# Moving an unused 480-byte gap from in front of the streamed weight sums to in front of the ring of operands

## The chip, the cores and the metric

The kernel runs on one core of one Trainium2 chip. The metric is the device time of one execution in microseconds (us), lower is better. Times of a kernel are medians of several executions; the profile shows one more execution of its own.

## The reference

The reference is one transformer layer in float32 on x of shape (4, 1024, 256): attention with 16 heads of 16 and binarised weights, then a feed-forward part with ternary weights. The feed-forward part is what the change touches:

```python
def _tlin(x, w, s):
    return jnp.einsum('bsi,oi->bso', x, w) * s
h = jax.nn.silu(_tlin(x, w1_w, w1_s)) * _tlin(x, w2_w, w2_s)     # 256 -> 1024
h = jax.nn.gelu(_tlin(h, h1_w, h1_s), approximate=False)         # 1024 -> 1024
h = jax.nn.gelu(_tlin(h, h2_w, h2_s), approximate=False)         # 1024 -> 1024
return _tlin(h, w3_w, w3_s)                                      # 1024 -> 256
...
x = x + _layernorm(_L0_attn_ref(_layernorm(x, axis=-1), ...), axis=-1)
x = x + _layernorm(_L0_ffn_ref(_layernorm(x, axis=-1), ...), axis=-1)
```

## The kernel before

The kernel has three parts, one after the other: `project` (the first tokens' projections), `attention` (the rest of it, about half of the time) and `tail_ffn` (output projection, layer norms and the feed-forward part). The tiles that the change moves exist only in `tail_ffn`; no tile of the first two parts changes its place.

`tail_ffn` goes through the 4096 tokens in 8 blocks of 512. TensorE runs an order of work that is written out by hand (`step`): 16 tiles of the first layer (`first_tile`, lines 1831 and 1832), then for each of the two hidden 1024 x 1024 layers 7 products of half size by Strassen's scheme in Winograd's form (`product`, line 1893), then the last layer (`out_part`, line 1906). In the first hidden layer the output projection of the next block (`project_y`, line 1798) stands between two products, and 8 transposes (`turn_x1`, line 1806) stand inside the last layer.

Numbers with all bits of float32 are given to TensorE as a high and a low part (tile `op_hi`, and `op_lo` as the rest), so each weight tile is used by two matmuls in a row. ScalarE makes `op_hi` (line 2008), VectorE makes `op_lo` (line 2148), into a ring of three slots each, 4096 bytes per partition and slot. One product is 32 matmuls (2 halves, 4 k-tiles, 2 output tiles, 2 parts), each with a stationary tile of 128x128 and a moving tile of 256 columns:

```python
w = weights(l, k, kt, 2 * h + a)
for part in (op_hi, op_lo):
    mm = pe.matmul(dst[:, a * HB:(a + 1) * HB], w, part[slot][:, kt // 2, cols].bitcast(form), ...)
```

With 14 products in each of 8 blocks that makes 14 x 32 = 448 matmuls of line 1893 in a block and 3584 in the program. 4 of 7 products read their weights from `W`, which stays in SBUF; 3 of 7 read them from `sums_of_w`, two tiles of 8192 bytes that are streamed from DRAM by SyncE's queue.

A trace writes the moving operand first and the stationary one second: `ffn_ps<-op_hi,W` is a matmul whose moving operand is `op_hi` and whose weights come from `W`. In line 1906 the roles are exchanged (`ffn_ps<-W,op_hi`): there `op` is stationary and `W` moves.

**Where the tiles lie.** The program allocates SBUF in order, each tile after the one before it; the byte address in each partition follows from the sizes. Slices are whole multiples of 512 bytes from their tile's start (128 columns of 4 bytes), so what can tell two uses apart is the start modulo 512:

```
tile                       start     modulo 512   used by TensorE in lines
signs_p                    16512     128          1798 (moving)
W                          24736     160          1831, 1832, 1893 (stationary), 1906 (moving)
x_hi0 of project           82592     160          697 (moving)
x2_hi, x2_lo               131232    160          1831, 1832 (moving), 1798, 1203, 1205 (stationary)
feed0, feed1               143552    192          -
op_hi0..2, op_lo0..2       176320    192          1893 (moving), 1906 (stationary)
gap (480 bytes, unused)    200896    -            -
sums_of_w0, sums_of_w1     201376    160          1893 (stationary)
signs                      223200    480          697, 698 (stationary), 1203, 1205 (moving)
```

(In the trace the names `x_hi` and `x_lo` stand for `x2_hi` and `x2_lo` too, which `attention` uses in lines 1203 and 1205.)

Of the kernel before, what the change touches and what calls it, by code (L numbers as in the profile page):

```python
# [6 lines left out]
F32 = mybir.dt.float32  # L7
# [7 lines left out]
P = 128  # L15
# [216 lines left out]
def layer(nc, x, attn_w, attn_wT, attn_b, attn_b_rows, ffn_w, ffn_s, ffn_s3, out):  # L232
# [14 lines left out]
    with ExitStack() as keep, ExitStack() as until_ffn:  # L247
# [57 lines left out]
        attention(nc, c, qk_scr, v_scr, m_scr, y_scr, ffn_w, w_scr, sum_scr, W, quads, first, x, tail_in, inv_scr, spent)  # L305
        until_ffn.close()
        tail_ffn(nc, x, y_scr, sum_scr, inv_scr, c, W, tail_in, out)


# [1260 lines left out]
def tail_ffn(nc, x, y_scr, sum_scr, inv_scr, const, W, tail_in, out):  # L1570
# [9 lines left out]
    with ExitStack() as ctx:  # L1580
        def sb(name, shape, dt):
            return ctx.enter_context(nc.sbuf_tensor(name, shape, dt))
# [6 lines left out]
        y_hi, y_lo = x2_hi, x2_lo  # L1589
        feed = [sb(f"feed{l}", [P, 4, 2, BLK], F32) for l in range(LAYERS)]  # L1590
        RING = 3
        op_hi = [sb(f"op_hi{r}", [P, 2, BLK], F32R) for r in range(RING)]
        op_lo = [sb(f"op_lo{r}", [P, 2, BLK], F32R) for r in range(RING)]
        SHIFTED = 480
        sb("gap", [P, SHIFTED // 4], F32)
        sums = [sb(f"sums_of_w{u}", [P, HK, HM], F32R) for u in range(2)]
        gate = [sb(f"gate{a}", [P, BLK], F32) for a in range(2)]
        o_sb = sb("o_sb", [P, TILES, DIM], F32)
# [80 lines left out]
        def op_at(i, l, k):  # L1679
            return OPS * i + NP * l + k + 1  # L1680
# [109 lines left out]
        def _(pe):  # L1790
# [87 lines left out]
            def product(i, l, k):  # L1878

                slot, fresh = (NP * l + k) % RING, k in (K_C11, K_C11_END, K_Z)  # L1880
                pe.wait_ge(op_lo_done, op_at(i, l, k))
# [17 lines left out]
            def out_part(i, dst, r, s, a, first, last):  # L1899
# [5 lines left out]
                for part in (op_hi, op_lo):  # L1905
                    mm = pe.matmul(dst, part[o % RING][:, s // 2, tokens].bitcast(form), w,  # L1906
                                   start=(first and part is op_hi), stop=(last and part is op_lo))
# [60 lines left out]
        def _(act):  # L1968
# [22 lines left out]
            def wait_slot(i, o):  # L1991

                old = o - RING if o >= RING else o - RING + OPS
                old_i = i if o >= RING else i - 1
                if isinstance(old_i, int) and old_i < 0:
# [385 lines left out]
```

## Time and profile before

| what | value |
|---|---|
| median of 3 runs | 1169.46 us (1166.7 to 1173.56) |
| the profiled execution's own time | 1167.74 us |
| its span, first to last instruction | 1166.0 us |
| granted TensorE clock, mean | 0.992 of full speed |
| TensorE busy | 1130.3 us, 97% of the span |
| ScalarE busy | 922.5 us, 79% |
| VectorE busy | 749.4 us, 64% |

The profiled execution took 1.74 us more than its span (what lies before the first and after the last instruction). Matmuls are pipelined: each is recorded with its whole passage (some 280 ns for 256 columns), and the next one starts before it has ended. What a matmul costs is therefore the distance from its start to the next one's start, which this text calls its step; it is read from the chain (length of a piece by its count) or from start times in the timeline.

### The profile page before, as it was taken

What the parts mean: (1) busy time and instruction counts of PE and PEld (TensorE: products, weight loads), DVE (VectorE), ACT (ScalarE), POOL (GpSimd) and SP (SyncE); (2) the same over time, 40 slices, a digit from 0 to 9 for tenths busy, and PEclk for the clock granted to TensorE, in tenths of its full rate; (3) what the DMA queues carried; (4) which work ended last, traced back from release to release, by engine and by line L of the source; (5) the groups of instructions that cost most, each with busy time, mean ns of one, the idle gap of its engine ahead of it and who ended that gap; (6) DMA issues with size and microseconds to landing.
All of it is one profiled execution on the core that took longest, in us unless ns stands there. A gap on an engine that the chain in (4) does not pass through costs nothing.

```text
span 1166.0 us, 21113 instructions
## 1 busy us (share of the span) xinstructions
PE 1130.3 (97%) x8241; PEld 769.6 (66%) x8241; DVE 749.4 (64%) x1162; ACT 922.5 (79%) x1218; POOL 97.0 (8%) x140
## 2 busy tenths in 40 slices
PE   6699999999999999998999999999999999999997
PEld 4233333333333322324999999999999999999997
DVE  8354524363345436795876878768778687687666
ACT  6689999999999999996676676667756766677665
POOL 6001000101010100010010000010100000101000
PEclk9799999999999999999999999999999999999999
DMA  5989768996879859954332430433324314333031
GB/s 187 242 213 236 189 101 188 219 224 105 166 166 198 178 97 224 266 159 174 109 110 76 145 128 22 153 137 109 113 71 145 128 32 168 113 109 131 15 127 56
DMA packets 67319, 167.03 MB, mean 143 GB/s; under 512 B 10390, under 2 KB 27414, under 8 KB 61062
## 3 DMA queue, kind: packets, MB, share of 16 engines
q1 hardware_dynamic: 66924, 165.18, 52.9%
q8 instruction: 70, 1.15, 0.4%
q10 hardware_dynamic: 288, 0.39, 0.2%
q14 instruction: 37, 0.30, 0.1%
HBM read 122.21 MB, written 52.43 MB: 150 GB/s over the span
## 4 chain that ended last, share of the span: by engine, by line
PE 52%; DVE 1%; issue 0%; ACT 0%; ACTq 0%
PE ffn_ps L1893 36%; PE ffn_ps L1831 5%; PE ffn_ps L1832 5%; PE ffn_ps L1906 5%; PE side_ps L1798 1%; PE side_ps L1806 1%; DVE ln_stats L2242 0%; DVE o_sb L2253 0%; DVE o_sb L2250 0%; DVE o_sb L2240 0%; ACT op_hi L2008 0%; DVE ln_mean_var L2244 0%; DVE ln_rstd L2248 0%; DVE op_lo L2148 0%; ACTq L2001 0%
## 5 line engine op out<-in xcount | busy, mean ns | idle before, releaser
L1308 ACT ACTIVATE probs<-s_ps 128x1024 f32<-128x1024 f32 x512 | 475.3, 1140 | 29.0 <-PE s_ps L1153 28.2
L1167 PE MATMUL y_ps<-probs,v_st 128*17 128x512 f32 x2048 | 270.3, 600 | 4.3 <-ACT probs L1308 2.1
L1893 PE MATMUL ffn_ps<-op_hi,W 128*128 128x256 f32 x1024 | 240.4, 279 | 0.0
L1893 PE MATMUL ffn_ps<-op_lo,W 128*128 128x256 f32 x1024 | 240.4, 279 | 0.0
L1153 PEld LDWEIGHTS s_ps<-q_st,k_st 50*128 50x128 f32 x1024 | 88.1, 185 | 208.9 <-ACT probs L1308 171.9
L2148 DVE TENSOR_TENSOR op_lo<-feed,op_hi 128x1024 fp32r<-128x1024 f32 x144 | 175.3, 1222 | 67.7 <-ACT op_hi L2008 67.6
L1153 PE MATMUL s_ps<-q_st,k_st 50*128 50x512 f32 x1024 | 207.1, 469 | 8.4 <-DMA q_st<-shift 7.9
L1893 PEld LDWEIGHTS ffn_ps<-op_lo,W 128*128 128x128 f32 x1024 | 192.6, 188 | 0.3
L1893 PEld LDWEIGHTS ffn_ps<-op_hi,W 128*128 128x128 f32 x1024 | 192.4, 188 | 0.3
L2008 ACT ACTIVATE op_hi<-feed 128x1024 fp32r<-128x1024 f32 x144 | 151.2, 1055 | 50.0 <-DVE feed L2166 21.9
L1893 PE MATMUL ffn_ps<-op_lo,sums_of_w 128*128 128x256 f32 x768 | 180.7, 279 | 0.0
L1893 PE MATMUL ffn_ps<-op_hi,sums_of_w 128*128 128x256 f32 x768 | 180.6, 279 | 0.0
L1893 PEld LDWEIGHTS ffn_ps<-op_lo,sums_of_w 128*128 128x128 f32 x768 | 144.5, 188 | 0.0
L1893 PEld LDWEIGHTS ffn_ps<-op_hi,sums_of_w 128*128 128x128 f32 x768 | 144.3, 188 | 0.0
L2037 ACT ACTIVATE feed<-feed,scales 128x256 f32<-128x256 f32 x192 | 86.9, 501 | 29.8 <-DVE feed L2191 15.1
L1831 PE MATMUL ffn_ps<-x_hi,W 128*128 128x512 f32 x256 | 99.8, 390 | 2.8 <-issue 2.8
L1832 PE MATMUL ffn_ps<-x_lo,W 128*128 128x512 f32 x256 | 99.7, 389 | 0.0
L1975 ACT ACTIVATE gate<-ffn_ps,scales 128x512 f32<-128x512 f32 x64 | 43.9, 688 | 64.3 <-PE ffn_ps L1832 64.3
L1167 PEld LDWEIGHTS y_ps<-probs,v_st 128*17 128x17 f32 x2048 | 34.5, 95 | 82.0 <-issue 72.6
L1333 DVE COPY y_sb<-y_ps 128x512 f32<-128x512 f32 x32 | 22.1, 690 | 103.1 <-PE y_ps L1167 103.1
L2141 DVE SCALAR_TENSOR_TENSOR feed<-ffn_ps,scales,gate 128x512 f32<-128x512 f32 x64 | 47.0, 747 | 32.3 <-PE ffn_ps L1832 32.3
L1906 PE MATMUL ffn_ps<-W,op_hi 128*128 128x256 f32 x256 | 62.0, 284 | 0.6 <-DVE op_lo L2148 0.6
(207 smaller groups left out, 1310.0 us busy)
## 6 DMA issues: line engine op xcount, KB each, us to landing
sums_of_w<-sum_scr SPq DMA_DIRECT2D x48, 1024.0 KB, 5.1
k_st<-qk_scr SPq DMA_DIRECT2D x90, 128.0 KB, 6.6
q_st<-qk_scr SPq DMA_DIRECT2D x90, 128.0 KB, 7.1
w_scr<-ffn_w SPq DMA_DIRECT2D x16, 704.0 KB, 7.8
W<-w_scr SPq DMA_DIRECT2D x16, 704.0 KB, 5.9
y_scr<-y_sb SPq DMA_DIRECT2D x32, 256.0 KB, 2.9
qk_scr<-y SPq DMA_DIRECT2D x24, 256.0 KB, 6.8
qk_scr<-sums SPq DMA_DIRECT2D x24, 256.0 KB, 7.7
```

The costliest lines, as they stand in the source:

```text
L1153: i = pe.matmul(s_ps[a % 3][:, hh, :], k_st[u][rows, pp, s * P:(s + 1) * P], q_st[u][rows, pp, tb * BLK:(tb + 1) * BLK], start=True, stop= ...
L1167: i = pe.matmul(y_ps[32 * j:32 * j + VCOLS, :], v_st[g % 2][:, s, VCOLS * j:VCOLS * (j + 1)], probs[(PAIRS * turn + j // 2) % PROBS][:, j ...
L1308: act.activation(probs[a % PROBS][:, :, :], s_ps[a % 3][:, :, :], ACT.Exp, scale=SCALE)\
L1831: pe.matmul(dst, w, x2_hi[:, c, :].bitcast(form), start=(c == 0), stop=False)
L1832: mm = pe.matmul(dst, w, x2_lo[:, c, :].bitcast(form), start=False, stop=(c == CT - 1))
L1893: mm = pe.matmul(dst[:, a * HB:(a + 1) * HB], w, part[slot][:, kt // 2, cols].bitcast(form), start=(fresh and kt == 0 and a == 0 and part ...
L1906: mm = pe.matmul(dst, part[o % RING][:, s // 2, tokens].bitcast(form), w, start=(first and part is op_hi), stop=(last and part is op_lo))
L1975: act.activation(gate[n % 2][:, :], bank[BANK_ORDER[2 * n % 6]][:, :], ACT.Silu, scale=scales[:, S1_AT + n:S1_AT + n + 1]).then_inc(gate_d ...
L2008: act.activation(op_hi[o % RING][:, :, :], operand(o), ACT.Copy).then_inc(op_hi_done, 1)
L2037: g = act.activation(dst[:, cols], src[:, cols], ACT.Gelu, scale=scales[:, at:at + 1])
L2141: dve.scalar_tensor_tensor(dst, bank[BANK_ORDER[(2 * n + 1) % 6]][:, :].rearrange("p (j t) -> p j t", j=2), scales[:, S2_AT + n:S2_AT + n ...
L2148: dve.tensor_tensor(op_lo[o % RING][:, :, :], operand(o), op_hi[o % RING][:, :, :].bitcast(F32), ALU.subtract)\
```

## The change

The 480 bytes that no instruction reads or writes are allocated ahead of the ring `op_hi`, `op_lo` and no longer behind it. The ring's six slots lie 480 bytes higher (176800 and not 176320, so 160 and not 192 modulo 512). `sums_of_w` and all tiles behind it stay where they were, as do `W`, `feed` and all tiles ahead of the ring. No instruction, wait, semaphore or transfer is added, removed or put in another order.

```diff
         feed = [sb(f"feed{l}", [P, 4, 2, BLK], F32) for l in range(LAYERS)]
         RING = 3
+        SHIFTED = 480
+        sb("gap", [P, SHIFTED // 4], F32)
         op_hi = [sb(f"op_hi{r}", [P, 2, BLK], F32R) for r in range(RING)]
         op_lo = [sb(f"op_lo{r}", [P, 2, BLK], F32R) for r in range(RING)]
-        SHIFTED = 480
-        sb("gap", [P, SHIFTED // 4], F32)
         sums = [sb(f"sums_of_w{u}", [P, HK, HM], F32R) for u in range(2)]
```

## Rows read from the trace of the kernel before

**Rows 1.** The page, part 1: engine, busy us (share of the span), instructions.
```profile
PE 1130.3 (97%) x8241; PEld 769.6 (66%) x8241; DVE 749.4 (64%) x1162; ACT 922.5 (79%) x1218; POOL 97.0 (8%) x140
```

**Rows 2.** The chain that ended last, one block: start us, us, what, count.
```profile
558.35 18.67 PE ffn_ps L1893 x160
577.01 1.88 PE side_ps L1798 x16
578.90 33.61 PE ffn_ps L1893 x288
612.50 3.78 PE ffn_ps L1906 x32
616.29 0.87 PE side_ps L1806 x8
617.16 3.79 PE ffn_ps L1906 x32
...
635.50 18.67 PE ffn_ps L1893 x160
```

**Rows 3.** Windows of two whole blocks: stretch, us, then busy us of each engine.
```profile
558.33:635.48 77.15, 77.15 (x603) 74.62 (x602) 57.72 (x79) 51.74 (x82) 7.07 (x12) 1.00 0.30 104
...
635.48:712.63 77.15, 77.15 (x603) 74.61 (x602) 58.86 (x80) 53.70 (x86) 7.14 (x12) 1.00 0.33 111
```

**Rows 4.** Groups by line from 543.5 us on: busy, mean ns | idle before.
```profile
L1893 PE MATMUL ffn_ps<-op_hi,W 128*128 128x256 f32 x1024 | 240.4, 279 | 0.0
L1893 PE MATMUL ffn_ps<-op_lo,W 128*128 128x256 f32 x1024 | 240.4, 279 | 0.0
...
L1893 PE MATMUL ffn_ps<-op_lo,sums_of_w 128*128 128x256 f32 x768 | 180.7, 279 | 0.0
L1893 PE MATMUL ffn_ps<-op_hi,sums_of_w 128*128 128x256 f32 x768 | 180.6, 279 | 0.0
L2148 DVE TENSOR_TENSOR op_lo<-feed,op_hi 128x1024 fp32r<-128x1024 f32 x144 | 175.3, 1222 | 67.7 <-ACT op_hi L2008 67.6
L2008 ACT ACTIVATE op_hi<-feed 128x1024 fp32r<-128x1024 f32 x144 | 151.2, 1055 | 50.0 <-DVE feed L2166 21.9 <-DVE feed L2141 17.7 <-DVE feed L2159 5.2
...
L1906 PE MATMUL ffn_ps<-W,op_hi 128*128 128x256 f32 x256 | 62.0, 284 | 0.6 <-DVE op_lo L2148 0.6
```

**Rows 5.** Timeline of TensorE in a product, W and then sums_of_w stationary.
```profile
799.79 0.28 PE L1893 MATMUL ffn_ps<-op_lo,W 128*128 128x256 f32 x1
...
800.73 0.28 PE L1893 MATMUL ffn_ps<-op_lo,W 128*128 128x256 f32 x1
800.85 0.28 PE L1893 MATMUL ffn_ps<-op_hi,sums_of_w 128*128 128x256 f32 x1
...
802.95 0.28 PE L1893 MATMUL ffn_ps<-op_hi,sums_of_w 128*128 128x256 f32 x1
```

**Rows 6.** Timeline of TensorE in the first layer, 512 columns.
```profile
547.76 0.39 PE L1831 MATMUL ffn_ps<-x_hi,W 128*128 128x512 f32 x1
...
549.12 0.39 PE L1831 MATMUL ffn_ps<-x_hi,W 128*128 128x512 f32 x1
```

**Rows 7.** Timeline of TensorE in project, 512 columns.
```profile
20.29 0.39 PE L697 MATMUL qk_ps<-x_hi,signs 128*128 128x512 f32 x1
...
21.69 0.39 PE L697 MATMUL qk_ps<-x_hi,signs 128*128 128x512 f32 x1
```

**Rows 8.** Timeline of TensorE in attention, two times the same work.
```profile
213.44 0.28 PE L1205 MATMUL p_ps<-signs,x_lo 128*128 128x256 f32 x1
...
214.12 0.28 PE L1205 MATMUL p_ps<-signs,x_lo 128*128 128x256 f32 x1
...
209.00 0.28 PE L1205 MATMUL p_ps<-signs,x_lo 128*128 128x256 f32 x1
...
209.71 0.28 PE L1205 MATMUL p_ps<-signs,x_lo 128*128 128x256 f32 x1
```

**Rows 9.** Lines 2048 and 2199: min/median/max ns of writes into x2_hi, x2_lo.
```profile
L2048 ACT ACTIVATE x_hi<-y x7: 1044/1046/1049, 570.6 to 1033.5; 128x1024 fp32r<-128x1024 f32 x7
...
L2199 DVE TENSOR_TENSOR x_lo<-y,x_hi x7: 1224/1226/1227, 571.7 to 1034.6; 128x1024 fp32r<-128x1024 f32 x7
```

## The prediction

> **What bounds the kernel now.** I read the page first: TensorE is busy for 97% of the span, VectorE and ScalarE for 64% and 79% [rows 1]. Then the chain that ended last. From 543.5 us on it is TensorE alone, piece after piece without a gap, until the last layer norm; one block is 18.67 + 1.88 + 33.61 + 3.78 + 0.87 + 3.79 us and the first layer's 14.5 us, and the next block starts its products 77.15 us later [rows 2]. The windows of two blocks say the same: TensorE busy in all of the 77.15 us, VectorE in 58.9, ScalarE in 53.7 [rows 3], and the groups show no idle time ahead of line 1893 and 0.6 us in all ahead of line 1906 [rows 4]. So in this part of the program the time is the number of matmuls times their step, and no wait of another engine decides. The change can only count if it alters the duration of instructions: it moves no work and no order.
>
> Next, the steps. In the products a piece of 288 matmuls takes 33.61 us and one of 160 takes 18.67 us: both 116.7 ns each [rows 2]. 256 columns at the full clock of 2.4 GHz would be 106.7 ns, so each step holds 10.0 ns more. The timeline shows the same step with `W` (8 steps in 0.94 us, 117.5, rounded) and with `sums_of_w` (18 steps in 2.10 us, 116.7) [rows 5]. All ring slots, k-tiles and output tiles lie in these pieces, and the step is the same for all; so if the address counts, it is by what they have in common: the place modulo 512 bytes.
>
> **The change part by part.** (1) Moved: the six slots of the ring, from 192 to 160 modulo 512. Let D be the start of the stationary operand less that of the moving one, modulo 512. For the 3584 matmuls of line 1893 D is 160 - 192 = -32 before and 0 after. For the 512 of line 1906 (op stationary, `W` moving) it is 192 - 160 = +32 before and 0 after. Lines 1798, 1831 and 1832 keep their D (+32 and 0). (2) Not changed: `sums_of_w` and what lies behind it, and all DMAs, waits and queues.
>
> What does the step depend on? The trace has these classes:
> - 256 columns, D = -32: 116.7 ns, 10.0 over the columns' time [rows 2].
> - 256 columns, D = +32: line 1906 takes 3.78 us for 32, 118.1 ns; line 1798, with other tiles (moving at 128, stationary at 160), 1.88 us for 16, 117.5 ns [rows 2]. Between 0.8 and 1.4 ns above the products.
> - 256 columns, D = 160 - 480 = +192: the same code in two states, 6 steps in 0.68 us (113.3 ns) and 6 in 0.71 us (118.3 ns) [rows 8].
> - 512 columns, D = 0: 6 steps in 1.36 us, 226.7 ns, 13.3 over 213.3 [rows 6].
> - 512 columns, D = 480 - 160 = -192: 6 steps in 1.40 us, 233.3 ns, 20.0 over 213.3 [rows 7].
>
> The two 512-column classes have the same shape and the same kind of loop (a weight tile used for a high and a low part), and differ by 6.7 ns a step. The operands' places are the visible difference, which makes me believe that D counts at all; the steady levels stand 3.3 ns apart or a multiple of it (113.3, 116.7; 226.7, 233.3). I take it that the reading of the next weights and the reading of the moving columns get in each other's way, more or less according to D.
>
> The price of D = 0 with 256 columns is in no row, so it is bounded. Below: the shortest step of that width, 113.3 ns [rows 8], is also half of the 512-column step at D = 0 (226.7 / 2 = 113.3) [rows 6]; if the extra time goes with the columns, each matmul gains 3.33 ns, 3584 x 3.33 = 11.9 us less. Above: if the extra time belongs to one weight load (128 columns of weights in both widths), it is 13.3 ns here as in rows 6, so 106.7 + 13.3 = 120.0 ns, 3584 x 3.33 = 11.9 us more. Between: the neighbour at D = +32 is 1.4 ns dearer than the one at D = -32, 3584 x 1.4 = 5.0 us if D = 0 behaves like it. I take the upper value. With 256 columns the weight load, which overlaps the matmul before it, has no slack left: a disturbed load holds up the next matmul, whereas with 512 columns it is hidden, so the narrow matmul should pay at least what the wide one pays. It is also the next level above the present one.
>
> Line 1906 goes from 118.1 to 120.0 as well: 512 x 1.9 = 1.0 us more (below: 512 x 4.8 = 2.5 us less). Sum: 11.9 + 1.0 = 12.9 us.
>
> What is written to the ring costs nothing in either case. The 144 writes each of ScalarE (1055 ns) and VectorE (1222 ns) [rows 4] have twins that write into tiles at 160 modulo 512 from an unmoved source: 1046 and 1226 ns [rows 9], 9 ns less and 4 ns more; all of it lies under TensorE, with 77.15 - 58.86 = 18.3 us of room on VectorE in a block [rows 3]. If that cover were gone, it would be 144 x 4 ns = 0.6 us. Even with a TensorE block 1.5 us shorter (448 x 3.33 ns) VectorE stays under it, so a gain would arrive in full.
>
> A page of the Trainium skill speaks against all this. TensorE: Matmul & The Clock Gate, section Back-to-back issue gap, has a step of the columns at 2.4 GHz and some 2.5 ns, with no term for an address; by it the step would be an estimated 109.2 ns before and after and the sum zero. The trace does not agree with its size (116.7 ns) [rows 2], nor with one extra for both 512-column classes [rows 6, 7]. SBUF — State Buffer, section SBUF: two separate sides, says that TensorE's reads never wait for another engine; that fits the even steps, and would leave the ring's move without effect on what ScalarE and VectorE do to TensorE.
>
> **The sum against the times.** The profiled execution took 1167.74 us; 1167.74 + 12.9 = 1180.6 us. The median of the runs shown is 1.7 us above it, 1182.3 us with the same sum. I say 1180.5.
>
> **The rivals.**
> - The step rises, but only to that of the neighbours at D = +32: 3584 x 1.4 = 5.0 us, 1173 us. For it speak the two lines of that class [rows 2]; against it that they don't hold one level, as the steady classes do.
> - No change: D does not set the step, but the loop's order, or the state that a stretch falls into (the same code gave 113.3 and 118.3 ns [rows 8], with D the same). Time 1167.7 to 1169.5 us. For it: `W` and `sums_of_w` cost the same; but they have the same D. Against it: rows 6 against rows 7.
> - The other side: faster. The two read streams are best aligned when they start at the same place, and the extra goes with the columns: steps of 113.3 ns, 11.9 us less in line 1893 and 2.5 us less in line 1906, 14.4 us, 1153.3 us; with line 1893 alone 1155.8 us. For it: rows 6 have the lower of the two 512-column levels, and 113.3 is a state that does occur. It decides once the mean step of line 1893 falls below 115.0 ns (3584 x 1.63 = 5.8 us, 0.5%).
>
> **How the numbers follow.** Full rise to 120 ns: 0.42. Small rise, by 2 to 8 us: 0.16. No change: 0.22. Faster: 0.20. A measurement of this kernel can tell about 0.5% (5.8 us) from no change. Slower by over 0.5%: the 0.42 and 0.06 of the small rises, 0.48. Within 0.5%: 0.22 and the other 0.10 of the small rises, 0.32. Faster: 0.20. The range goes from 1157 us, which takes in most cases of a gain in line 1893 alone, to 1186 us, the likeliest case on the median (1182.3) and the spread of the runs; the likeliest one's own range is 1176 to 1186 us.
>
> **What would show it.** In the chain of the changed kernel the piece of 160 matmuls of line 1893 tells all: 18.67 us now, 19.20 us if the step is 120.0, 18.13 us if it is 113.3; the block of 77.15 us becomes 78.8 or 75.4. The first layer's pieces of 226.7 ns, line 1798, and everything ahead of 543.5 us should not move. The prediction is wrong if the step stays at 116.7 ns, or if `W` and `sums_of_w` get different steps, which would mean that it isn't D that counts; and it fails on its sign if the extra goes with the columns.

## The result, and the profile after

| | before | after |
|---|---|---|
| median of 6 runs each | 1168.28 us | 1182.03 us |
| the profiled execution's own time | 1167.74 us | 1181.85 us |
| its span | 1166.0 us | 1180.1 us |

The ratio is 1.0101, 95% interval 1.0079 to 1.0122: the kernel became slower by 1.0%. The forecast was 1180.5 us.

The page of the kernel after, part 1 (engine, busy us, share of the span, instructions), against [rows 1]:

```profile
PE 1145.5 (97%) x8241; PEld 783.7 (66%) x8241; DVE 749.7 (64%) x1162; ACT 923.8 (78%) x1218; POOL 96.8 (8%) x140
```

The instructions are the same in number; TensorE is busy for 15.2 us more, VectorE and ScalarE for 0.3 and 1.3 us more. The chain that ended last, one block of the kernel after (start us, us, what, count), against [rows 2]:

```profile
796.16 19.19 PE ffn_ps L1893 x160
815.35 1.90 PE side_ps L1798 x16
817.25 34.54 PE ffn_ps L1893 x288
851.79 3.84 PE ffn_ps L1906 x32
855.64 0.87 PE side_ps L1806 x8
856.51 3.83 PE ffn_ps L1906 x32
...
874.87 19.19 PE ffn_ps L1893 x160
```

The reader is to divide: 19.19 us by 160 and 34.54 us by 288 are 119.9 ns, where there were 116.7. Line 1906 went from 3.78 and 3.79 us to 3.84 and 3.83. Line 1806 and the first layer kept their times, and line 1798 (1.90 us for 1.88) nearly so. The timeline of one product after, 18 steps from its 13th matmul on:

```profile
640.00 0.28 PE L1893 MATMUL ffn_ps<-op_hi,W 128*128 128x256 f32 x1
...
642.16 0.28 PE L1893 MATMUL ffn_ps<-op_hi,W 128*128 128x256 f32 x1
```

2.16 us for 18 steps: 120.0 ns. (Start times are printed to 0.01 us, so a step read over 18 of them is good to some 0.6 ns.) A window of 78.7 us, which is a block of the kernel after, against [rows 3]:

```profile
721.00:799.70 78.70, 78.70 (x602) 76.19 (x601) 58.88 (x81) 53.86 (x87) 7.12 (x12) 1.00 0.32 109
```

TensorE is still without a gap, VectorE and ScalarE do the same work in more time. The difference of the spans is 14.1 us. It is made of 7 blocks that begin 78.71 us and not 77.15 us apart (10.9 us), the 448 matmuls of the last block in 53.75 and not 52.27 us (1.5 us), and 1.7 us by which the first product begins later (560.02 for 558.35 us). The last part is no work of the change. Windows of both kernels at the start of the first layer (the last three columns are the granted clock, the DMA share and GB/s); before:

```profile
540.00:545.00 5.00, 2.18 (x14) 1.24 (x7) 0.69 (x1) 1.51 (x2) 0.17 (x3) 1.00 0.45 128
545.00:550.00 5.00, 5.00 (x23) 4.13 (x22) 1.50 (x2) 1.84 (x3) 0.00 (x0) 1.00 0.91 365
```

and after:

```profile
540.00:545.00 5.00, 2.19 (x15) 1.08 (x8) 0.69 (x1) 1.28 (x1) 0.17 (x3) 0.84 0.40 108
545.00:550.00 5.00, 5.00 (x20) 4.02 (x19) 1.50 (x2) 1.38 (x2) 0.00 (x0) 0.81 0.95 379
```

TensorE was busy for less than half of the first of these windows in both (2.18 and 2.19 of 5.00 us), and in the execution profiled after it was granted the lower of its two clocks, 1.2 GHz, for some 3 us. Five steps of the first layer took 0.43 us each there, which is 512 columns at 1.2 GHz:

```profile
544.39 0.63 PE L1832 MATMUL ffn_ps<-x_lo,W 128*128 128x512 f32 x1
...
546.53 0.56 PE L1831 MATMUL ffn_ps<-x_hi,W 128*128 128x512 f32 x1
```

The experiments below show that this isn't the work of the change: the profiled executions of eight of their twelve kernels had such a stretch at this place and four had none, and the two kernels with the whole ring at D = +64 and +320, which are alike in all else, are one of each (granted clock 0.68 and 1.00 from 545 to 550 us).

### The profile page after: what moved, and what is told of

Read it like the earlier page. It is cut to its first block, busy times and chain, and to the rows that moved or that the text cites. A ratio compares the mean times of both kernels' runs of the same rounds, so it can differ in the third digit from the quotient of the medians.

```text
span 1180.1 us, 21113 instructions
## 1 busy us (share of the span) xinstructions
PE 1145.5 (97%) x8241; PEld 783.7 (66%) x8241; DVE 749.7 (64%) x1162; ACT 923.8 (78%) x1218; POOL 96.8 (8%) x140
## 4 chain that ended last, share of the span: by engine, by line
PE 53%; DVE 1%; issue 0%; ACT 0%; ACTq 0%
PE ffn_ps L1893 36%; PE ffn_ps L1831 5%; PE ffn_ps L1832 5%; PE ffn_ps L1906 5%; PE side_ps L1798 1%; PE side_ps L1806 1%; DVE ln_stats L2242 0%; DVE o_sb L2253 0%; DVE o_sb L2250 0%; DVE o_sb L2240 0%; ACT op_hi L2008 0%; DVE ln_mean_var L2244 0%; DVE ln_rstd L2248 0%; DVE op_lo L2148 0%; ACTq L2001 0%
## 5 line engine op out<-in xcount | busy, mean ns | idle before, releaser
L1893 PE MATMUL ffn_ps<-op_lo,W 128*128 128x256 f32 x1024 | 247.0, 283 | 0.0
L1893 PE MATMUL ffn_ps<-op_hi,W 128*128 128x256 f32 x1024 | 247.0, 283 | 0.0
L2148 DVE TENSOR_TENSOR op_lo<-feed,op_hi 128x1024 fp32r<-128x1024 f32 x144 | 175.3, 1222 | 69.3 <-ACT op_hi L2008 68.4
L1893 PEld LDWEIGHTS ffn_ps<-op_lo,W 128*128 128x128 f32 x1024 | 196.4, 192 | 0.3
L1893 PEld LDWEIGHTS ffn_ps<-op_hi,W 128*128 128x128 f32 x1024 | 196.4, 192 | 0.3
L2008 ACT ACTIVATE op_hi<-feed 128x1024 fp32r<-128x1024 f32 x144 | 151.1, 1055 | 49.2 <-DVE feed L2166 21.9
L1893 PE MATMUL ffn_ps<-op_hi,sums_of_w 128*128 128x256 f32 x768 | 185.7, 283 | 0.0
L1893 PE MATMUL ffn_ps<-op_lo,sums_of_w 128*128 128x256 f32 x768 | 185.7, 283 | 0.0
L1893 PEld LDWEIGHTS ffn_ps<-op_hi,sums_of_w 128*128 128x128 f32 x768 | 147.5, 192 | 0.0
L1893 PEld LDWEIGHTS ffn_ps<-op_lo,sums_of_w 128*128 128x128 f32 x768 | 147.5, 192 | 0.0
```

The costliest lines, as they stand in the source:

```text
L2008: act.activation(op_hi[o % RING][:, :, :], operand(o), ACT.Copy).then_inc(op_hi_done, 1)
L2148: dve.tensor_tensor(op_lo[o % RING][:, :, :], operand(o), op_hi[o % RING][:, :, :].bitcast(F32), ALU.subtract)\
```

## The experiments

The question left by the prediction was whether the step of a matmul is set by D (the start of its stationary operand less that of its moving one, modulo 512), and at which value of D it takes how long. Each fence shows, for one kernel, the first and the last of 19 matmuls in a product of the second block, so the distance of the two start times is 18 steps.

**Split: the gap of after, and a second one in front of the sums.**

```diff
         SHIFTED = 480
         sb("gap", [P, SHIFTED // 4], F32)
         op_hi = [sb(f"op_hi{r}", [P, 2, BLK], F32R) for r in range(RING)]
         op_lo = [sb(f"op_lo{r}", [P, 2, BLK], F32R) for r in range(RING)]
+        sb("gap2", [P, 480 // 4], F32)
```

> The kernel of the change with a second gap of 480 bytes in front of sums_of_w: ring at 160, W at 160 (D = 0), sums_of_w at 128 modulo 512 (D = -32). Theory (the step of line 1893 is set by D): 120.0 ns in the 2048 matmuls with W, 116.7 ns in the 1536 with sums_of_w, line 1906 at 120.0; 2048 x 3.33 = 6.8 us and 1 us for line 1906 over the kernel before, about 1176 us. Rival A (it is the place of the ring by itself, now an odd multiple of 32 bytes, that costs): 120.0 ns in both, as after the change, about 1181 us. Rival B (any move of the sums away from 160 matters): sums_of_w gets a level other than these two.

Median 1177.61 us, ratio to before 1.006 (1.0037 to 1.0084). The timeline, first a product with `W`, then one with `sums_of_w`:

```profile
637.40 0.28 PE L1893 MATMUL ffn_ps<-op_hi,W 128*128 128x256 f32 x1
...
639.56 0.28 PE L1893 MATMUL ffn_ps<-op_hi,W 128*128 128x256 f32 x1
...
648.88 0.28 PE L1893 MATMUL ffn_ps<-op_hi,sums_of_w 128*128 128x256 f32 x1
...
650.99 0.28 PE L1893 MATMUL ffn_ps<-op_hi,sums_of_w 128*128 128x256 f32 x1
```

120.0 ns with `W` and 117 ns (2.11 / 18) with `sums_of_w`, from the same ring. Rival A, the ring's place by itself, is out, and so is rival B, a new level for the moved `sums_of_w`: 117 ns is the level of D = -32.

**No gap at all.**

```diff
         op_lo = [sb(f"op_lo{r}", [P, 2, BLK], F32R) for r in range(RING)]
-        SHIFTED = 480
-        sb("gap", [P, SHIFTED // 4], F32)
```

> No gap at all: ring at 192 and W at 160 as in the kernel before (D = -32), sums_of_w at 192 (D = 0). Theory: 116.7 ns with W, 120.0 ns with sums_of_w, line 1906 as before at about 118.2; 1536 x 3.33 = 5.1 us over the kernel before, about 1173.5 us. Rival A (place of the ring by itself): ring unmoved, so 116.7 ns in both and the time of before.

Median 1174.53 us, ratio 1.0029 (1.0016 to 1.0043). The timeline:

```profile
638.24 0.28 PE L1891 MATMUL ffn_ps<-op_hi,W 128*128 128x256 f32 x1
...
640.34 0.28 PE L1891 MATMUL ffn_ps<-op_hi,W 128*128 128x256 f32 x1
...
649.47 0.28 PE L1891 MATMUL ffn_ps<-op_hi,sums_of_w 128*128 128x256 f32 x1
...
651.63 0.28 PE L1891 MATMUL ffn_ps<-op_hi,sums_of_w 128*128 128x256 f32 x1
```

Now `W` has 116.7 ns and `sums_of_w` 120.0. D = 0 costs 120.0 ns with both operands at 160 and with both at 192, D = -32 costs 117 with 192 and 160 as with 160 and 128: the difference counts, the places don't.

**Three values of D in one kernel: each slot of the ring at its own place.** `op_hi` and `op_lo` of a slot have the same place modulo 512; the gaps are `(352, 64, 32)` ahead of the three high slots, `(416, 64, 32)` ahead of the low ones and 32 ahead of the sums, in the first of three such kernels:

```diff
-        op_hi = [sb(f"op_hi{r}", [P, 2, BLK], F32R) for r in range(RING)]
-        op_lo = [sb(f"op_lo{r}", [P, 2, BLK], F32R) for r in range(RING)]
+        def placed(name, gap):
+            if gap:
+                sb(f"gap_{name}", [P, gap // 4], F32)
+            return sb(name, [P, 2, BLK], F32R)
+
+        op_hi = [placed(f"op_hi{r}", gap) for r, gap in enumerate((352, 64, 32))]
+        op_lo = [placed(f"op_lo{r}", gap) for r, gap in enumerate((416, 64, 32))]
```

> Each slot of the ring at its own place: slot 0 at 32, slot 1 at 96, slot 2 at 128 modulo 512, W and sums_of_w at 160, so D = +128, +64, +32. Product number n of a block uses slot n modulo 3. Theory: the step depends on the slot and is the same for W and sums_of_w in it; slot 2 takes about 118.2 ns without one steady level, as line 1906 did at D = +32; the other two are open, 113.3 to 118.3. Rival A (the place by itself: multiples of 64 are good, odd multiples of 32 bad): all three of one kind except slot 2 (128), which has 116.7, the others 120.0. Rival C (only the equality D = 0 costs): all three at 116.7.

The timeline, slots 0, 1 and 2:

```profile
647.77 0.28 PE L1898 MATMUL ffn_ps<-op_hi,sums_of_w 128*128 128x256 f32 x1
...
649.91 0.28 PE L1898 MATMUL ffn_ps<-op_hi,sums_of_w 128*128 128x256 f32 x1
...
651.50 0.28 PE L1898 MATMUL ffn_ps<-op_hi,sums_of_w 128*128 128x256 f32 x1
...
653.54 0.28 PE L1898 MATMUL ffn_ps<-op_hi,sums_of_w 128*128 128x256 f32 x1
...
657.08 0.28 PE L1898 MATMUL ffn_ps<-op_hi,W 128*128 128x256 f32 x1
...
659.21 0.28 PE L1898 MATMUL ffn_ps<-op_hi,W 128*128 128x256 f32 x1
```

118.9 ns at D = +128, 113.3 at +64, 118.3 at +32. Rivals A and C are out. Of slot 0 this is the level in all products but the first of each block, which took 120.0 ns a step (from 636.51 to 638.67 us for 18 steps), so D = +128 has two levels. The execution's own time, 1167.77 us, is that of before to 0.1 us, and its pieces of 160 and 288 matmuls take 18.70 and 33.61 us: three levels that differ by 5 ns add up to the old sum, which no view by line would have told apart.

**The next three values**, with gaps `(160, 64, 64)`, `(384, 64, 64)` and 192.

> Slot 0 of the ring at 352, slot 1 at 416, slot 2 at 480 modulo 512: D = -192 (320), +256, +192. Theory: slot 2 takes 113.3 or 117.7 ns, the two states that the 256-column matmuls at D = +192 show in attention; slot 0 is dearer than slot 2, since the 512-column matmuls at D = -192 are 6.7 ns dearer than those at D = 0, so 120 ns or more; slot 1 is open. Rival A (place by itself): slots 1 and 2 (multiples of 32 that are odd or even alike) follow only whether the place is a multiple of 64: slots 0, 1 and 2 all odd multiples of 32, so 120.0 in all. Rival C (only D = 0 costs): 116.7 in all.

The timeline, slots 2, 0 and 1:

```profile
646.69 0.28 PE L1898 MATMUL ffn_ps<-op_hi,W 128*128 128x256 f32 x1
...
648.81 0.28 PE L1898 MATMUL ffn_ps<-op_hi,W 128*128 128x256 f32 x1
...
650.41 0.28 PE L1898 MATMUL ffn_ps<-op_hi,sums_of_w 128*128 128x256 f32 x1
...
652.45 0.28 PE L1898 MATMUL ffn_ps<-op_hi,sums_of_w 128*128 128x256 f32 x1
...
654.10 0.28 PE L1898 MATMUL ffn_ps<-op_hi,sums_of_w 128*128 128x256 f32 x1
...
656.26 0.28 PE L1898 MATMUL ffn_ps<-op_hi,sums_of_w 128*128 128x256 f32 x1
```

117.8 ns at D = +192 as expected, 120.0 at +256. At +320 it was 113.3 here and 117.8 in other products; I had expected 120 or more, from the 512-column matmuls at the same D [rows 7]. That was wrong.

**Three more, two of them equal modulo 256**, with gaps `(320, 64, 256)`, `(192, 64, 256)` and 352.

> Slot 0 of the ring at 0, slot 1 at 64, slot 2 at 320 modulo 512: D = +160, +96, and +352, which is +96 once more modulo 256. The runs so far gave 120.0 ns at D = 0 and mostly at +256, 113.3 at +64 and partly at -192 (+320, the same modulo 256). Theory, narrowed: the step depends on D modulo 256, so slots 1 and 2 take the same within 0.7 ns; slot 0 is open, between 116.7 and 120. Rival (modulo 512 and not less): slots 1 and 2 more than 1 ns apart.

The timeline, slots 0, 1 and 2:

```profile
669.42 0.28 PE L1898 MATMUL ffn_ps<-op_hi,sums_of_w 128*128 128x256 f32 x1
...
671.58 0.28 PE L1898 MATMUL ffn_ps<-op_hi,sums_of_w 128*128 128x256 f32 x1
...
673.22 0.28 PE L1898 MATMUL ffn_ps<-op_hi,W 128*128 128x256 f32 x1
...
675.34 0.28 PE L1898 MATMUL ffn_ps<-op_hi,W 128*128 128x256 f32 x1
...
676.98 0.28 PE L1898 MATMUL ffn_ps<-op_hi,W 128*128 128x256 f32 x1
...
679.09 0.28 PE L1898 MATMUL ffn_ps<-op_hi,W 128*128 128x256 f32 x1
```

120.0 ns at D = +160, 117.8 (2.12 / 18) at +96 and 117.2 (2.11 / 18) at +352. The pair agrees within the 0.7 ns that was set. Other products are dearer: from 648.52 to 650.66 us slot 1 took 118.9 ns (2.14 / 18). Both slots of the pair have these two levels, 117.3 and 118.7 ns over longer stretches; the lower one comes in the three of their products that follow line 1798 next, the higher one in all others and in the whole last block, and level by level the two slots agree. With +64 and +320, and 0 and +256, that makes three pairs. (This kernel's own time, 1183.06 us, holds a stretch of the lower clock at the start of the first layer, longer than the one above, and is not used.)

**The best value for the whole ring.**

```diff
+        sb("gap0", [P, 416 // 4], F32)
         op_hi = [sb(f"op_hi{r}", [P, 2, BLK], F32R) for r in range(RING)]
         op_lo = [sb(f"op_lo{r}", [P, 2, BLK], F32R) for r in range(RING)]
-        SHIFTED = 480
-        sb("gap", [P, SHIFTED // 4], F32)
+        sb("gap", [P, 64 // 4], F32)
```

> The whole ring at 96 modulo 512 (416 bytes of gap in front of it, 64 in front of the sums): D = +64 for all of line 1893. Theory: 113.4 ns in all 3584 matmuls, 3584 x 3.3 = 11.8 us less than before, about 1157 us, ratio 0.990. Rival (the 113.3 ns of one slot came from the slots beside it, with other places, and is a state that a stretch falls into): 116 to 118 ns, ratio 0.997 to 1.003.

and with 160 and 320 bytes in place of 416 and 64:

> The whole ring at 352 modulo 512: D = +320 (-192) for all of line 1893, the same as +64 modulo 256. Theory modulo 256: 113.3 to 115.3 ns (the slot at this D had stretches of 113.3 and of 117.8), ratio 0.990 to 0.995. Theory modulo 512: its own level, 115 to 120 ns. It also sets the 256-column matmul beside the 512-column one at the same D, which took 233.3 ns, 20.0 ns over its columns: if narrow matmuls paid at least what wide ones pay, as the prediction argued, this one would take 126.7 ns and the ratio be 1.03.

D = +64: 1164.55 us, ratio 0.9949 (0.9930 to 0.9968). D = +320: 1164.01 us, ratio 0.9936 (0.9915 to 0.9957). Both beat both kernels, the first by half of what was expected. The chain of the second, block two and the last block, says why:

```profile
633.76 18.85 PE ffn_ps L1893 x160
652.61 1.89 PE side_ps L1798 x16
654.50 32.67 PE ffn_ps L1893 x288
...
1091.72 52.77 PE ffn_ps L1893 x448
```

117.8 ns in the 160 matmuls ahead of line 1798, 113.4 in the 288 behind it, and 117.8 in all 448 of the last block, where line 1798 does not occur. At D = +64 the pieces are the same (18.84, 32.67 and 52.77 us). So there are two states at this D, and a stretch keeps one of them for hundreds of matmuls. (Behind line 1798 the first five steps still took 118 to 123 ns; only then did the short state begin.) For D = +320 the mean over all products is 115.3 ns, within the 113.3 to 115.3 that was expected of a period of 256 bytes. The rival of 126.7 ns is out.

Line 1906 has D = +192 in this kernel (modulo 512), and it too has two levels, directly behind the short products and behind the transposes of line 1806:

```profile
687.18 3.63 PE ffn_ps L1906 x32
...
691.68 3.77 PE ffn_ps L1906 x32
```

That is 113.4 and 117.8 ns, near the two values of attention at the same D [rows 8].

**Is it so for 512 columns?** The tile `x2_hi` and all behind it are allocated 32 bytes higher, with ring and sums at their old places modulo 512.

```diff
-            x2_hi=sb("x2_hi", [P, CT, BLK], F32R),
+            x2_hi=(sb("gap_x2", [P, 32 // 4], F32), sb("x2_hi", [P, CT, BLK], F32R))[1],
...
+        sb("gap0", [P, 480 // 4], F32)
         op_hi = [sb(f"op_hi{r}", [P, 2, BLK], F32R) for r in range(RING)]
```

> The ring and the sums as in the kernel before (D = -32), but the moving tiles x2_hi and x2_lo of the 512-column matmuls at 192 modulo 512 and not 160, so D = -32 for lines 1831 and 1832 and +64 for line 1798; the tiles of attention behind them lie 32 bytes higher. Theory: the 512-column step leaves 226.7 ns (more likely up, to 230 or 233.3: 512 x 3.3 to 6.7 = 1.7 to 3.4 us), line 1798 goes from 117.7 to 113.4 ns, line 1893 stays at 116.7. Rival (D matters for narrow matmuls only, where the weight load has no slack): 226.7 ns as before.

The timeline, 11 steps of the first layer:

```profile
630.52 0.40 PE L1831 MATMUL ffn_ps<-x_hi,W 128*128 128x512 f32 x1
...
633.09 0.40 PE L1832 MATMUL ffn_ps<-x_lo,W 128*128 128x512 f32 x1
```

233.6 ns, up from 226.7 [rows 6]. The chain has the products' pieces at 18.67 and 33.60 us, unchanged, and line 1798, now at D = +64, at 1.84 us for 16 (115.0 ns for 117.5; 113.4 was expected). The rival, that D matters for narrow matmuls only, is out, and for wide ones D = 0 is the cheap value. (That it is D and not the new place of `x2_hi` by itself was shown for the narrow ones only.)

**Half of each weight load.** Each matmul of line 1893 uses 64 of its 128 weight columns, so it also writes 64 output partitions and not 128: the kernel leaves out half of the hidden layers.

```diff
-                                mm = pe.matmul(dst[:, a * HB:(a + 1) * HB], w, part[slot]...
+                                mm = pe.matmul(dst[0:HALF, a * HB:(a + 1) * HB], w[:, 0:HALF], part[slot]...
```

> Line 1893 with 64 columns of each weight tile and not 128 (its output fills 64 of 128 partitions; half of the hidden layers is left out), moving columns unchanged at 256. Slot 0 at D = +64, slot 1 at +32, slot 2 at 0. Theory (the extra time is the weight load and the moving columns getting in each other's way): with half the weights to read the extra over 106.7 ns falls, at D = 0 from 13.3 to 6.7 ns or less (113.3), and the slots come together. Rival (the extra belongs to each matmul and its moving operand's place, whatever is loaded beside it): 120.0 ns in slot 2 and 118.2 in slot 1 as with full tiles.

The timeline, slots 0, 1 and 2 (128*64 is the stationary tile):

```profile
638.27 0.28 PE L1897 MATMUL ffn_ps<-op_hi,W 128*64 128x256 f32 x1
...
640.41 0.28 PE L1897 MATMUL ffn_ps<-op_hi,W 128*64 128x256 f32 x1
...
642.05 0.28 PE L1897 MATMUL ffn_ps<-op_hi,W 128*64 128x256 f32 x1
...
644.15 0.28 PE L1897 MATMUL ffn_ps<-op_hi,W 128*64 128x256 f32 x1
...
645.76 0.28 PE L1897 MATMUL ffn_ps<-op_hi,W 128*64 128x256 f32 x1
...
647.80 0.28 PE L1897 MATMUL ffn_ps<-op_hi,W 128*64 128x256 f32 x1
```

At D = 0 the step fell from 120.0 to 113.3 ns, at +32 from 118.3 to 116.7; at +64 it rose, from 113.3 or 117.8 to 118.9. The moving operands and their places are those of full tiles, so the rival is out: the extra time does not hang on the moving operand alone. It goes with the weight tile's width, be it by what is loaded or by the output, which was halved with it; the run does not tell these apart. But "half the load, half the extra" holds at D = 0 alone; the order of the three values of D is turned round, and the slots did not come together.

**Trying for the short state from the start.** First one added matmul of 128 columns in front of each block's products:

```diff
+                    if l == 0 and k == K_C11 and h == 0:
+                        pe.matmul(dst[:, 0:P], weights(l, k, 0, 0), op_hi[slot][:, 0, 0:P].bitcast(form), start=True, stop=True)
```

> The whole ring at D = +320 again, and in front of the first product of each block one added matmul of 128 columns whose output the first real one overwrites. At D = +64 and +320 the first five products of each block took 117.8 ns, the later nine 113.3, the switch came where the output projection of the next block (line 1798) stands between two products, and in the last block, which has none, all fourteen stayed at 117.8. Theory: a stretch of equal matmuls keeps the state that it entered in, and something of another shape in between lets it enter anew; the added matmul makes the first product enter at 113.3 ns: 7 x 5 x 32 x 4.5 ns + 14 x 32 x 4.5 ns = 7.1 us less than the kernel with D = +320 alone, less 8 x 0.11 us, ratio to the kernel before about 0.988. Rival: which state it enters depends on more than that, the first five products stay at 117.8 ns, and the ratio stays at 0.994.

1165.30 us, ratio 0.9957 (0.9940 to 0.9975). The pieces are 18.90, 32.67 and 52.82 us: ahead of line 1798 and in the last block the long state stayed. The rival held. Then a ring with slot 0 at D = -32 (gaps `(0, 160, 0)`, `(352, 160, 0)` and 320):

> Slot 0 of the ring at 192 modulo 512 (D = -32), slots 1 and 2 at 352 (D = +320). Theory: slot 0 takes 116.7 ns and, being of another D, lets slot 1 enter anew, so slots 1 and 2 take 113.3 throughout, the last block too: 1280 x 116.7 and 2304 x 113.3, 7.7 us less than before, ratio 0.9935. Rival: slot 1 enters at 117.8 ns after slot 0, and the time is that of before or above.

1166.45 us, ratio 0.9959 (0.9942 to 0.9975). The chain, last two blocks:

```profile
1020.88 18.78 PE ffn_ps L1898 x160
...
1041.55 33.05 PE ffn_ps L1898 x288
...
1097.51 52.60 PE ffn_ps L1898 x448
```

The last block's 52.60 us are 160 x 116.7 and 288 x 117.8 ns (18.7 + 33.9), so slots 1 and 2 stayed in the long state there although slot 0, at another D, stands between them; behind line 1798 they were in the short one. Lastly four matmuls at D = +32, the D of line 1798, in front of each block's products, with the ring at D = +320:

```diff
+                    if l == 0 and k == K_C11 and h == 0:
+                        for n in range(4):
+                            pe.matmul(dst[:, 0:HB], weights(l, k, n, 0), const.signs_p[:, 0, :].bitcast(form), start=(n == 0), stop=(n == 3))
```

> The whole ring at D = +320, and in front of the first product of each block four added matmuls of 256 columns with W stationary (160 modulo 512) and signs_p moving (128), so D = +32 as in line 1798, whose 16 matmuls are what stands between the products at 117.8 ns and those at 113.3; the first real matmul overwrites their output. Theory (a stretch at another D of the same width lets the products enter the short state, which a single 128-column matmul at D = +320 did not): the first five products and all of the last block take 113.3 ns; 7.1 us less than with D = +320 alone, 32 x 0.118 = 3.8 us for the added ones, ratio to the kernel before about 0.991. Rival (four are not enough, or the entry depends on something else): the first five products stay at 117.8 ns, and the ratio rises to 0.997.

1167.47 us, ratio 0.9973 (0.9957 to 0.9989), pieces of 18.84, 32.67 and 52.76 us. The long state stayed, and the added matmuls cost what they take. My theory of the entry fell with these three runs.

## Why the prediction was right

**What bounds the kernel.** Right. TensorE has no gap in the tail before or after, so each ns of a step arrived in full; VectorE and ScalarE kept their durations (1222 and 1055 ns each in their 144 writes) and stayed under TensorE, as costed.

**D sets the step.** Right, and shown: split and no gap gave 120.0 ns to whichever weights stood at D = 0, with the ring moved or not. The rival of no change, that the loop's order or a chance state makes the levels, is out as the cause of this change. It was right about one thing: at D = +64 and +320, and at +96, +128 and +192 as well, there are two levels. What the prediction took for a period of 512 bytes is one of 256, where three pairs were tried.

**The size.** 120.0 ns was forecast and 120.0 measured: 11.9 us forecast for line 1893, and 7 x 1.46 + 1.48 = 11.7 us found (the block's two pieces are 0.52 and 0.94 us longer). For line 1906 1.0 us was forecast and 0.10 us a block, 0.8 us in all, found. So 12.5 us were found for a sum of 12.9. The span grew by 14.1 us, of which 1.7 us lie ahead of the first product; they are the clock's.

**The reasons for the size.** Here the number was better than its argument, and in part luck. The step "the narrow matmul should pay at least what the wide one pays" failed. At D = +320 the narrow one pays 6.7 or 11.1 ns over its columns and the wide one 20.0 [rows 7]. At D = 0 both pay 13.3 ns, which is why the rule hit. Its ground, that a disturbed load is hidden beside 512 columns, did not shelter the wide one: its step rose from 226.7 to 233.6 ns when its moving tile lay 32 bytes higher. "The next level above the present one" was no reason: steady steps of 117.8 and 118.7 ns exist between 116.7 and 120.0. The lower bound (the extra goes with the columns, 113.3 ns) was wrong for the change, which keeps 128 weight columns beside 256 moving ones. With 64 beside 256, the proportion of 128 beside 512, D = 0 does cost 113.3 ns, half of 226.7 [rows 6]; but at D = +64 the half tile takes 118.9 ns, where half of the wide step at the same D modulo 256 is 116.7 (233.3 / 2) [rows 7]. So neither bound is a rule, and no row of the kernel before could have priced D = 0; the 0.42 that the forecast gave to its own case was deserved. Of the interpolation from the neighbours (118.1 ns at D = +32, 116.7 at -32) the runs show that D = 0 does not lie between them.

**The rule of the page.** The Trainium skill, TensorE: Matmul & The Clock Gate, section Back-to-back issue gap, has no term for an address, neither in its formula for a matmul by itself, which the prediction used, nor in what it says of streams of weight loads and matmuls, and by it nothing would have changed. With 256 columns and unchanged instructions the runs span 113.3 to 120.0 ns; the measurement decides.

**What stays open.** That the reading of the next weights and the reading of the moving columns disturb each other fits all of this: the step depends on the difference of their places, and on the width of the weight tile. It was not shown, and the form of such a conflict was not found. Nor was what decides between 113.3 and 117.8 ns at D = +64: behind the 16 matmuls of line 1798 the short state came every time, behind one or four added matmuls, or 32 at D = -32, it did not. Behind the 32 matmuls at D = +128 of the first three-place ring it came in all products but one (a product of the fifth block that began behind steps of 0.40 and 0.19 us stayed at 117.8 ns), behind those at +192 of the second only in some products.

The steps found, narrow ones with a full weight tile, in ns (the first column of each pair is D modulo 256):

```
D      0      32     64             96             128            160    192            224 (-32)
step   120.0  118.3  113.3 / 117.8  117.3 / 118.7  118.7 / 120.0  120.0  113.4 / 117.8  116.7
```

(Where two values stand, both are levels that whole products, or whole pieces of line 1906, kept. Those at 96 and 128 are read over longer stretches than the 18 steps above and so differ a little from them. The 113.4 ns at 192 are line 1906's; the ring took 117.8 there in every product.)

## What to carry to other kernels

Where TensorE runs without gaps, its step per matmul is a number worth reading to a tenth of a ns: two loops of one shape that differ by 3 ns a step are not noise, and over 3584 matmuls such 3 ns are 12 us. The difference of the start addresses of the stationary and the moving tile, modulo 256 bytes, is a free parameter: an unused gap of some hundred bytes was worth +1.0% or -0.6% here, and a ring with its slots at different places measures three values in one run. The best difference is not the same for another proportion of weight to moving columns (D = 0 was, with +160, the worst value for 128 beside 256, and the best of three for 128 beside 512), so it is to be measured for each shape and not carried over.

## What the runs showed of the hardware that was not expected

- The step of equal matmuls depends on D with a period of 256 bytes, and the order of the values turns round when the weight tile is halved: 120.0, 118.3 and 113.3 ns at D = 0, 32 and 64 with 128 weight columns, 113.3, 116.7 and 118.9 with 64.
- The same instructions at the same addresses have two steady steps at D = +64, 113.3 and 117.8 ns, and hold the long one over 448 matmuls and the short one over the 280 or so behind line 1798. D = +96, +128 and +192 have two levels as well, D = 0, +160 and -32 showed only one. Thirty-two matmuls at D = -32 in between, which take 116.7 ns themselves, don't end the long state.
- Differences cancel in sums: a ring with 118.9, 113.3 and 118.3 ns in its slots had the same pieces (18.70 and 33.61 us) as one with 116.7 ns throughout.
